# Second cross attention: heads scored in quads by row tiles, keys spread once a sequence, values in one block

## The chip, the core and the metric

The kernel runs on one core of a Trainium2 chip. The metric is the device time of one execution in microseconds (us): 3467.15 us is the median of three runs of the kernel before, from 3467.04 to 3475.69. TensorE (PE in the rows; PEld is its weight load), VectorE (DVE), ScalarE (ACT) and GpSimd (POOL) each run a queue of their own in order; they meet only at semaphores.

## The reference

A transformer decoder of two layers over 64 sequences of 128 tokens with 128 features. Six sublayers run one after the other, each on a layer norm of the residual x and added to x. The change touches the fifth, a cross attention with 16 heads of 8 features to a context of 77 positions per sequence, with a mask over the context:

```
x = x + L1_xattn(layernorm(x), ctx, ctx, mask, Wq, bq, Wk, bk, Wv, bv, Wo, bo)
# q = x @ Wq + bq; k, v = ctx @ Wk + bk, ctx @ Wv + bv; 16 heads of 8 features
# scores = q k^T / sqrt(8); masked positions get a very low score
# probs = softmax(scores); out = (probs v) @ Wo + bo
```

Everything is in 32-bit floating point.

## The kernel before

Each sublayer is a stage with a block of its own on every engine, and a barrier stands between stages. The stage of the change is `stage_context_attention`; its tiles have the prefix f_. It takes the 64 sequences one after the other (`over_sequences`: two steps, a loop of two steps a turn, four steps at the end), software-pipelined: step b works on sequence b, and prepares b+1, b+2 and b+3. Within a sequence the 16 heads are four groups of four: head 4g + u, with NG = 4 quads g and NU = 4 places u in a quad. Features 32g to 32g+31 belong to quad g.

For one group of four heads the kernel before does this, with n = 4b + u counting groups:

- `spread_keys` (GpSimd, line 2168) writes the keys of the sequence four times side by side, each copy zeroed outside the features of its head (`kx`, 128 x 308). One such instruction a group.
- `score` (TensorE, 1927 and 1929) puts the mask with an identity matmul in bf16 into a PSUM bank of `sc`, and adds q times the spread keys with a 32-bit matmul over all 128 features; a 32-bit matmul stands in the trace as two records. Two banks take turns.
- `lowest` (VectorE, 2023) finds the extreme of each head's row, `exponentials` (ScalarE, 2132) takes four exponentials with their sums, `invert` (VectorE, 2035) the reciprocal of the sums. The division is on GpSimd for even groups (`divide_even`, 2177), on VectorE for odd ones (`divide_odd`, 2042).
- `transposes` (TensorE, 1940) transposes the four heads into a bank of `tr`, of which there are two; `copy_probs` (ScalarE, 2141) copies it to SBUF; `values` (TensorE, 1951) multiplies by the values, in column tiles of 32, one group at a time.

Once a sequence there are also: `transpose_x`, `project_qk`, `project_v`, `project_out` (TensorE); `biases` (VectorE: the mask row `neg` 2000, `qT` 2002, `kT` 2006), `spread_values` (2015), `copy_out` (2051), `residual` (2056) and the layer norm of sequence b+3 (VectorE with GpSimd); `copy_xT` (ScalarE); `add_bias` (GpSimd).

The order on each engine is the order in which its `step` is written out by hand. A buffer that is used again is guarded by a wait on its last reader, for example `exponentials` of group n waits until the division of group n-2 has read `pr`.

Of the kernel before, what the change touches and what calls it, by code (L numbers as in the profile page):

```python
# [16 lines left out]
BF16 = mybir.dt.bfloat16  # L17
# [1806 lines left out]
def context_attention_weights(mem, w):  # L1824

    wT = mem.sbuf("wT", [128, 3, 128])
    woT = mem.sbuf("woT", [128, 128])
    bias = mem.sbuf("bias", [128, 2])
    bv = mem.sbuf("bv", [128, 128])
    bo = mem.sbuf("bo", [128, 128])  # L1830
    hsel = mem.sbuf("hsel", [128, H])
    mask = mem.sbuf("mask", [128, B, CK], I32)
    loads = [(wT[:], w["f_wT"]), (woT[:], w["f_woT"]), (bias[:], w["f_bias"]), (bv[:], bcast(w["f_bv"])),
            (bo[:], bcast(w["f_bo"])), (hsel[:], w["hsel"]),
            (mask[:].rearrange("p b k -> p (b k)"), bcast(w["mask"].rearrange("b k -> (b k)")))]
    return (wT, woT, bias, bv, bo, hsel, mask), loads


def stage_context_attention(nc, X, w, consts, tiles):
# [4 lines left out]

    KP = 96
    with ExitStack() as ctx:
        mem = Memory(nc, ctx, "f")
        wT, woT, bias, bv, bo, hsel, mask = tiles
# [8 lines left out]
        kx = mem.sbuf("kx", [128, 2, NU, NG, CK])  # L1857
        vx = mem.sbuf("vx", [128, 2, NU, 128])
        low = mem.sbuf("low", [128, 2, NG])
        sums = mem.sbuf("sums", [128, 2, NG])  # L1860
        rec = mem.sbuf("rec", [128, 2, NG])
        pr = mem.sbuf("pr", [128, 2, NG, CK])
        pn = mem.sbuf("pn", [128, 2, NG, KP])
        prT = mem.sbuf("prT", [128, 2, NG, 128])
        oT = mem.sbuf("oT", [128, 128])

        sc = mem.psum("sc", [128, 2, 512])
        tr = mem.psum("tr", [128, 2, 512])
# [12 lines left out]
        rec_made = mem.sem("rec_made")  # L1881
        pn_even, pn_odd = mem.sem("pn_even"), mem.sem("pn_odd")
        tr_made, prT_made = mem.sem("tr_made"), mem.sem("prT_made")
# [4 lines left out]
        with nc.Block() as block:  # L1888
# [10 lines left out]
            def _(pe):  # L1899
# [19 lines left out]
                def score(b, p, u):  # L1919
                    n = 4 * b + u  # L1920
                    if due(n - 1):
                        pe.wait_ge(exped, n - 1)
                    pe.wait_ge(neg_made, b + 1)
                    pe.wait_ge(qk_made, 2 * b + 2)
                    pe.wait_ge(kx_made, n + 1)
                    dst = sc[:, u % 2, 0:NG * CK]
                    pe.matmul(dst, consts.ident_bf[:], neg[:, p].unsqueeze(1).broadcast_to([128, NG, CK]),
                              start=True, stop=False)
                    pe.matmul(dst, qT[:, p], kx[:, p, u], start=False, stop=True).then_inc(scored, 1)

                def transposes(b, p, u):
                    n = 4 * b + u
                    if u % 2:
                        pe.wait_ge(pn_odd, 2 * b + u // 2 + 1)
                    else:
                        pe.wait_ge(pn_even, 2 * b + u // 2 + 1)
                    if due(n - 1):
                        pe.wait_ge(prT_made, n - 1)
                    for g in range(NG):
                        last = pe.transpose(tr[0:KP, u % 2, 128 * g:128 * g + 128], pn[:, u % 2, g], consts.ident[:])  # L1940
                    last.then_inc(tr_made, 1)

                def values(b, p, u):
                    pe.wait_ge(prT_made, 4 * b + u + 1)
                    if u == 0:
                        pe.wait_ge(vx_made, b + 1)
                        if due(b):
                            pe.wait_ge(oT_made, b)
                    for g in range(NG):
                        q = slice(32 * g, 32 * g + 32)  # L1950
                        last = pe.matmul(po[q, 0:128], vx[0:KP, p, u, q], prT[0:KP, u % 2, g],
                                         start=u == 0, stop=u == NU - 1, tile_position=(0, 32 * g))
                    last.then_inc(pv_made, 1)
# [7 lines left out]
                def step(b, p, last):  # L1961
                    if inside(b + 1):
                        project_v(b + 1, 1 - p)
                    for u in range(NU):
                        transposes(b, p, u)
                        if u == 0:
                            score(b, p, 3)
                        elif inside(b + 1):
                            score(b + 1, 1 - p, u - 1)
                        if u == 1 and inside(b + 2):  # L1970
                            transpose_x(b + 2, p)
                        if u == 2 and inside(b - 1):
                            project_out(b - 1)
                        if u == 2 and inside(b + 2):
                            project_qk(b + 2, p)
                        if u > 0:
                            values(b, p, u - 1)
                        elif inside(b - 1):
                            values(b - 1, 1 - p, NU - 1)
                    if last:  # L1980
                        values(b, p, NU - 1)
                        project_out(b)

                pe.wait_ge(ready, 3)
# [5 lines left out]
                for u in range(3):  # L1990
                    score(0, 0, u)
# [3 lines left out]
            def _(dve):  # L1995
                def biases(b, p):
# [7 lines left out]
                    if due(4 * b - 4):  # L2004
                        dve.wait_ge(kx_made, 4 * b - 4)
                    dve.tensor_scalar(kT[:, p], pf[:, 128:128 + CK], bias[:, 1:2], None, ALU.add).then_inc(qk_made, 1)

                def spread_values(b, p):
                    dve.wait_ge(v_made, b + 1)
                    if due(4 * b - 4):  # L2010
                        dve.wait_ge(pv_made, 4 * b - 4)
# [6 lines left out]
                def lowest(b, u):  # L2018
                    n = 4 * b + u
                    if due(n - 1):  # L2020
                        dve.wait_ge(exped, n - 1)
                    dve.wait_ge(scored, n + 1)
                    dve.tensor_reduce(low[:, u % 2], sc[:, u % 2, 0:NG * CK].rearrange("p (g k) -> p g k", g=NG),  # L2023
                                      AX.X, ALU.min).then_inc(low_found, 1)

                def invert(b, u):

                    n = 4 * b + u
                    if due(2 * b + u // 2):
                        if u % 2:  # L2030
                            dve.wait_ge(pn_odd, 2 * b + u // 2)
                        else:
                            dve.wait_ge(pn_even, 2 * b + u // 2)
                    dve.wait_ge(exped, n + 1)
                    dve.reciprocal(rec[:, u % 2], sums[:, u % 2]).then_inc(rec_made, 1)

                def divide_odd(b, u):
                    n = 4 * b + u
                    if due(n - 1):
                        dve.wait_ge(tr_made, n - 1)  # L2040
                    dve.wait_ge(rec_made, n + 1)
                    dve.tensor_tensor(pn[:, 1, :, 0:CK], pr[:, 1],
                                      rec[:, 1].unsqueeze(2).broadcast_to([128, NG, CK]), ALU.mult)\
                        .then_inc(pn_odd, 1)

                def copy_out(b):
# [3 lines left out]
                    dve.wait_ge(pv_made, 4 * b + 4)  # L2050
# [7 lines left out]
                def step(b, p, last):  # L2058

                    invert(b, 1)  # L2060
                    divide_odd(b, 1)
                    lowest(b, 3)
                    if inside(b - 1):
                        copy_out(b - 1)

                    invert(b, 2)
                    if inside(b + 3):
                        norm_statistics(dve, ln, X[:, b + 3], b + 3, 1 - p)
                    if inside(b + 1):
                        lowest(b + 1, 0)  # L2070
# [3 lines left out]

                    invert(b, 3)
                    divide_odd(b, 3)
                    if inside(b + 1):
                        lowest(b + 1, 1)
                    if inside(b - 1):
# [3 lines left out]

                    if inside(b + 1):
                        invert(b + 1, 0)
                        lowest(b + 1, 2)
                    if inside(b + 3):
                        dve.wait_ge(xT_made, b + 2)
                        norm_apply(dve, ln, X[:, b + 3], b + 3, 1 - p)
# [4 lines left out]
                dve.memset(vx[:], 0.0).then_inc(ready, 1)  # L2094
                dve.memset(pn[:], 0.0).then_inc(ready, 1)
                dve.tensor_scalar(allowed[:], mask[:], 0.0, None, ALU.not_equal).then_inc(ready, 1)
                dve.wait_ge(ready, 3)
# [11 lines left out]
                for u in range(3):  # L2109
                    lowest(0, u)  # L2110
                    if u == 0:
                        invert(0, 0)
# [3 lines left out]
            def _(act):  # L2116
# [6 lines left out]
                def exponentials(b, u):  # L2123
                    n = 4 * b + u
                    if due(2 * b + u // 2):
                        if u % 2:
                            act.wait_ge(pn_odd, 2 * b + u // 2)
                        else:
                            act.wait_ge(pn_even, 2 * b + u // 2)
                    act.wait_ge(low_found, n + 1)  # L2130
                    for g in range(NG):
                        op = act.activation(pr[:, u % 2, g], sc[:, u % 2, CK * g:CK * g + CK], ACT.Exp,  # L2132
                                            bias=low[:, u % 2, g:g + 1], scale=-1.0,
# [508 lines left out]
```

## Time and profile before

| | us |
|---|---|
| median of three runs | 3467.15 |
| the profiled execution | 3479.02 |
| span in the profile | 3477.2 |
| TensorE busy | 3171.6 (91%) |
| VectorE busy | 2570.1 (74%) |
| ScalarE busy | 2244.4 (65%) |
| GpSimd busy | 1567.5 (45%) |

The stage of the change stands between about 2600 and 3090 us of the span. The shares above are means over six stages, so the stage has to be read by itself: from its own stretch of the time line and its own groups. "Busy" joins the recorded durations; on TensorE the records of matmuls overlap and their ends are modelled, so the distance from one start to the next says more than the duration. In a row, "[0.62 <-PE f_sc L1929]" is the idle time of the engine ahead of the instruction and what ended it.

### The profile page before, as it was taken

The page shows a single profiled execution, that of the slowest core. Times are in us where ns is not written, and L with a number is a line of the kernel's source. Part 1 is how long each engine was busy: PE and PEld are TensorE (multiplying, and loading weights), DVE is VectorE, ACT ScalarE, POOL GpSimd, SP SyncE. Part 2 cuts the span into 40 slices and gives each one's busy share as a digit, 9 for nine tenths or more (in the row PEclk, how much of TensorE's full clock was granted, in tenths as well). Part 3 has the DMA queues.
Part 4 walks back from the last instruction along what each step waited for, and adds up shares of the span by engine and source line. Part 5 has one row for each costly group of instructions (what it writes and reads, how often), then busy time and mean ns, then how long its engine had stood idle before and what let it go on. Part 6 is the DMA issues. An engine that isn't in the chain of part 4 may idle for free. (4 is left out here: it accounts for less than half of the span.)

```text
span 3477.2 us, 97864 instructions
## 1 busy us (share of the span) xinstructions
PE 3171.6 (91%) x27203; PEld 2330.7 (67%) x27357; DVE 2570.1 (74%) x8326; ACT 2244.4 (65%) x8816; POOL 1567.5 (45%) x2572
## 2 busy tenths in 40 slices
PE   7999999899999999999999986879979999967776
PEld 4666666688888888888888864657756666644443
DVE  7888888577777777777777761126657888879997
ACT  6888888566666666666666652327758999952221
POOL 6888888312222222222222210016647777746665
PEclk9999999899999999999999998989999999977677
DMA  4000000100000000000000002220000000000000
GB/s 144 0 0 0 0 0 0 75 4 6 5 5 5 5 5 5 5 5 5 5 5 5 4 4 67 79 61 17 17 10 6 5 5 5 5 2 11 7 12 18
DMA packets 80366, 54.39 MB, mean 16 GB/s; under 512 B 24801, under 2 KB 74413, under 8 KB 80160
## 3 DMA queue, kind: packets, MB, share of 16 engines
q1 hardware_dynamic: 76192, 45.27, 4.6%
q0 software_dynamic: 4096, 8.16, 0.8%
q8 instruction: 39, 0.64, 0.1%
q14 instruction: 39, 0.32, 0.0%
HBM read 32.67 MB, written 20.97 MB: 15 GB/s over the span
## 5 line engine op out<-in xcount | busy, mean ns | idle before, releaser
L897 DVE COPY b_prT<-b_tr 128x512 f32<-128x512 f32 x512 | 352.2, 688 | 236.6 <-PE b_tr L789 232.3
L1155 ACT ACTIVATE b_pr<-b_sc,b_low 128x205 f32<-128x205 f32 x1024 | 430.3, 430 | 34.3 <-DVE b_low L873 34.3
L478 ACT ACTIVATE a_pr<-a_sc,a_low 128x128 f32<-128x128 f32 x1024 | 364.2, 381 | 37.2 <-POOL a_pn L522 26.3
L1212 POOL TENSOR_TENSOR b_ln_var<-b_ln_mean_var,all_eps 128x1 f32<-128x1 f32 x64 | 12.0, 187 | 756.6 <-DVE b_ln_mean_var L140 756.6
L888 DVE TENSOR_SCALAR b_pn<-b_pr,b_rec 128x205 f32<-128x205 f32 x1024 | 298.4, 334 | 54.8
L789 PE MATMUL b_tr<-all_ident,b_pn 128*128 128x128 f32 x2048 | 322.4, 280 | 5.3 <-DVE b_prT L897 3.1
L2132 ACT ACTIVATE f_pr<-f_sc,f_low 128x77 f32<-128x77 f32 x1024 | 319.1, 335 | 10.9 <-DVE f_low L2023 2.9
L513 POOL TENSOR_TENSOR a_kx<-a_qk,w_hsel 128x512 f32<-128x512 f32 x256 | 291.7, 1151 | 2.4 <-DVE a_qk L349 2.4
L789 PEld LDWEIGHTS b_tr<-all_ident,b_pn 128*128 128x128 f32 x2048 | 226.6, 140 | 86.9 <-issue 79.3
L265 PE MATMUL a_sc<-a_kx,a_qk 128*128 128x512 f32 x512 | 262.3, 594 | 11.7 <-POOL a_kx L513 9.2
L873 DVE TENSOR_REDUCE b_low<-b_sc 128x4 f32<-128x820 f32 x256 | 256.4, 1002 | 10.2 <-PE b_sc L777 10.2
L777 PE MATMUL b_sc<-b_kT,b_q 64*128 64x205 f32 x2048 | 247.0, 359 | 0.0
L478 ACT ACTIVATION_READ_ACCUMULATOR a_pr<-a_sc,a_low 128x1 f32 x1024 | 225.9, 221 | 0.0
L2132 ACT ACTIVATION_READ_ACCUMULATOR f_pr<-f_sc,f_low 128x1 f32 x1024 | 221.9, 217 | 0.0
L806 PE MATMUL b_pm<-b_prT,b_vt 128*64 128x128 f32 x2048 | 213.6, 284 | 8.3 <-issue 5.3
L276 PEld LDWEIGHTS a_tr<-all_ident,a_pn 128*128 128x128 f32 x1024 | 127.8, 141 | 135.0 <-issue 126.6
L1155 ACT ACTIVATION_READ_ACCUMULATOR b_pr<-b_sc,b_low 128x1 f32 x1024 | 208.6, 204 | 0.0
L806 PE MATMUL b_pm<-b_prT,b_vm 128*64 128x128 f32 x2048 | 202.2, 273 | 0.0
L487 ACT ACTIVATE a_prT<-a_tr 128x512 f32<-128x512 f32 x256 | 155.1, 606 | 67.9 <-PE a_tr L276 67.9
L367 DVE TENSOR_REDUCE a_low<-a_sc 128x4 f32<-128x512 f32 x256 | 173.6, 678 | 30.7 <-PE a_sc L265 30.2
L777 PEld LDWEIGHTS b_sc<-b_kT,b_q 64*128 64x128 f32 x2048 | 166.2, 186 | 43.7 <-issue 43.0
L1164 ACT ACTIVATE b_oT<-b_pm 128x256 f32<-128x256 f32 x256 | 97.5, 381 | 131.7 <-PE b_pm L806 130.3
(292 smaller groups left out, 8795.4 us busy)
## 6 DMA issues: line engine op xcount, KB each, us to landing
scratch_x<-b_zeros SPq DMA_DIRECT2D x12, 512.0 KB, 5.0
e_xr<-scratch_x SPq DMA_DIRECT2D x24, 256.0 KB, 3.0
scratch_y<-e_yr SPq DMA_DIRECT2D x24, 256.0 KB, 2.4
all_X<-in_x SPq DMA_DIRECT2D x8, 512.0 KB, 6.9
e_w<-in_e_w SPq DMA_DIRECT2D x16, 256.0 KB, 3.0
out_x<-all_X SPq DMA_DIRECT2D x8, 512.0 KB, 3.2
w_mask<-in_mask SPq DMA_DIRECT2D x1, 2464.0 KB, 9.8
b_cT<-in_ctxT SPq DMA_DIRECT2D x32, 77.0 KB, 2.0
```

Of the source, the lines that this page charges most:

```text
L265: pe.matmul(sc[:, u % 2], qk[:, p, 0], kx[:, p, u], start=False, stop=True).then_inc(scored, 1)
L367: dve.tensor_reduce(low[:, u % 2], sc[:, u % 2].rearrange("p (g k) -> p g k", g=NG), AX.X, ALU.min).then_inc(low_found, 1)
L478: op = act.activation(pr[:, u % 2, g], sc[:, u % 2, 128 * g:128 * g + 128], ACT.Exp, bias=low[:, u % 2, g:g + 1], scale=-1.0, accum_out=su ...
L513: pool.tensor_tensor(kx[:, p, u], qk[:, p, 1].unsqueeze(1).broadcast_to([128, NG, 128]), hsel[:, NG * u:NG * u + NG].unsqueeze(2).broadcas ...
L777: last = pe.matmul(sc[:, j % 2, h, KN * i:KN * i + KN], q[r, p, 2 * j + i], kT[r, p, 2 * j + i], start=True, stop=True, tile_position=(XD ...
L789: last = pe.transpose(tr[:, o:o + 128], pn[:, j % 2, 2 * i + h, 128 * t:128 * t + 128], consts.ident[:])
L806: last = pe.matmul(po[XD * h:XD * h + XD, 128 * i:128 * i + 128], v[:, p, f:f + XD], prT[:, j % 2, i, h, t], start=t == 0, stop=t == 1, ti ...
L873: dve.tensor_reduce(low[:, j % 2].rearrange("p (i h) -> p h i", h=2), sc[:, j % 2, :, 0:2 * KN].rearrange("p h (i k) -> p h i k", i=2), AX ...
L888: op = dve.tensor_scalar(pn[:, j % 2, g, 0:KN], pr[:, j % 2, g, 0:KN], rec[:, j % 2, g:g + 1], None, ALU.mult)
L897: dve.tensor_copy(prT[:, j % 2, i].rearrange("p h t q -> p (h t q)"), tr[:]).then_inc(prT_made, 1)
L1155: op = act.activation(pr[:, j % 2, g, 0:KN], sc[:, j % 2, h, KN * i:KN * i + KN], ACT.Exp, bias=low[:, j % 2, g:g + 1], scale=-1.0, accum_ ...
L2132: op = act.activation(pr[:, u % 2, g], sc[:, u % 2, CK * g:CK * g + CK], ACT.Exp, bias=low[:, u % 2, g:g + 1], scale=-1.0, accum_out=sums[ ...
```

## The change

In the new kernel the four heads that are worked on together are those of one quad g, so their features are one strip of 32 partitions.

- `score(b, p, half)` takes two quads at a time. Each quad is a row tile of 32 partitions with a PSUM bank of its own, four banks in all. The mask is added by a bf16 matmul over 32 partitions with a matrix `part` of 1/32.
- `spread_keys` runs once a sequence (`kx` is 128 x 308 for all four quads), with `own` in place of `hsel`.
- `transposes` writes into one bank `tr` instead of two. Its copy is on ScalarE for even quads (`copy_even`) and on VectorE for odd ones (`copy_odd`). `prT` holds all four quads of two sequences.
- `values` is one block of 16 matmuls a sequence, one step later than the transposes.
- All divisions are on GpSimd (`divide`).

The diff, cut to its core. On TensorE:

```diff
-                def score(b, p, u):
+                def score(b, p, half):
...
+                    for g in (2 * half, 2 * half + 1):
+                        q = slice(32 * g, 32 * g + 32)
+                        pe.matmul(sc[:, g, 0:NU * CK], part[q], neg[q, p].unsqueeze(1).broadcast_to([32, NU, CK]),
+                                  start=True, stop=False, tile_position=(32 * g, 0))
+                    for g in (2 * half, 2 * half + 1):
+                        q = slice(32 * g, 32 * g + 32)
+                        last = pe.matmul(sc[:, g, 0:NU * CK], qT[q, p], kx[q, p].rearrange("p u k -> p (u k)"),
+                                         start=False, stop=True, tile_position=(32 * g, 0))
+                    last.then_inc(scored, 2)
+                def transposes(b, g):
+                    n = 4 * b + g
+                    pe.wait_ge(normed, n + 1)
+                    if g % 2:
+                        pe.wait_ge(prT_even, n // 2 + 1 if isinstance(n, int) else 2 * b + g // 2 + 1)
+                    elif due(n):
+                        pe.wait_ge(prT_odd, 2 * b + g // 2)
...
                 def step(b, p, last):
+                    transposes(b, 0)
                     if inside(b + 1):
                         project_v(b + 1, 1 - p)
...
+                    if inside(b - 1):
+                        values(b - 1, 1 - p)
+                    transposes(b, 1)
+                    if inside(b + 1):
+                        score(b + 1, 1 - p, 0)
+                    transposes(b, 2)
+                    if inside(b + 2):
+                        transpose_x(b + 2, p)
+                    if inside(b + 1):
+                        score(b + 1, 1 - p, 1)
+                    transposes(b, 3)
+                    if inside(b - 1):
+                        project_out(b - 1)
+                    if inside(b + 2):
+                        project_qk(b + 2, p)
```

On VectorE, the copy that is new there (the step that calls it is shown as a queue below):

```diff
+                def copy_odd(b, p, g):
+                    if due(b - 1):
+                        dve.wait_ge(pv_made, b - 1)
+                    dve.wait_ge(tr_made, 4 * b + g + 1)
+                    dve.tensor_copy(prT[0:KP, p, g].rearrange("p u k -> p (u k)"), tr[0:KP]).then_inc(prT_odd, 1)
```

The step on ScalarE:

```diff
                 def step(b, p, last):
+                    exponentials(b, 2)
+                    copy_even(b, p, 0)
+                    exponentials(b, 3)
+                    if inside(b + 1):
+                        exponentials(b + 1, 0)
+                    copy_even(b, p, 2)
+                    if inside(b + 2):
+                        copy_xT(b + 2)
+                    if inside(b + 1):
+                        exponentials(b + 1, 1)
```

And the step on GpSimd:

```diff
                 def step(b, p, last):
+                    divide(b, 2)
                     if inside(b + 3):
                         norm_rsqrt(pool, ln, consts, b + 3, 1 - p)
+                    divide(b, 3)
+                    add_bias(b)
                     if inside(b + 1):
+                        divide(b + 1, 0)
                     if inside(b + 2):
+                        spread_keys(b + 2, p)
+                    if inside(b + 1):
+                        divide(b + 1, 1)
```

The guards follow the same pattern as before: `exponentials(n)` waits for `divide(n-2)`, `divide(n)` for the transposes of n-2, `transposes(n)` for the copy of n-1 out of `tr` (the wait above), `spread_keys(b)` for both `biases(b)`.

How this stands in the queues. First ScalarE before, the start of a step in the loop: exponentials of group 2, copy of 0, exponentials of 3, copy of 1.

```order
L2132 ACTIVATE f_pr,f_sums<-f_sc,f_low 128x77 x4
L2139 REGISTER_ALU
L2140 REGISTER_ALU
L2141 ACTIVATE f_prT<-f_tr 96x512
L2130 REGISTER_ALU
L2132 ACTIVATE f_pr,f_sums<-f_sc,f_low 128x77 x4
L2140 REGISTER_ALU
L2141 ACTIVATE f_prT<-f_tr 96x512
```

Now, the same place: exponentials (b, 2), copy (b, 0), exponentials (b, 3), exponentials (b+1, 0), copy (b, 2).

```order
L2126 ACTIVATE f_pr,f_sums<-f_sc,f_low 128x77 x4
L2132 REGISTER_ALU
L2134 ACTIVATE f_prT<-f_tr 96x512
L2123 REGISTER_ALU
L2124 REGISTER_ALU
L2126 ACTIVATE f_pr,f_sums<-f_sc,f_low 128x77 x4
L2123 ISA
L2124 REGISTER_ALU
L2126 ACTIVATE f_pr,f_sums<-f_sc,f_low 128x77 x4
L2134 ACTIVATE f_prT<-f_tr 96x512
```

Before, a copy stood behind each four exponentials; now the copy of quad 2 stands behind eight, the last four of which belong to the next sequence.

VectorE before, the end of a step's middle: division of group 3 (`f_pn`), `lowest`, `residual`, the three of `biases`, `invert` of the next sequence.

```order
L2042 TENSOR_TENSOR f_pn<-f_pr,f_rec 128x4x77
L2022 REGISTER_ALU
L2023 TENSOR_REDUCE f_low<-f_sc 128x4
L2056 ISA
L2056 TENSOR_TENSOR all_X<-f_pm,all_X 128x128
L1999 ISA
L2000 ISA
L2000 TENSOR_SCALAR f_neg<-f_allowed 128x77
L2002 TENSOR_SCALAR f_qT<-f_pf,w_bias 128x128
L2006 TENSOR_SCALAR f_kT<-f_pf,w_bias 128x77
```

Now, the end of a step: `copy_odd(b, 3)`, `lowest(b+1, 3)`, `invert(b+1, 1)`, `residual(b-1)` and `biases(b+2)`.

```order
L2042 COPY f_prT<-f_tr 96x512
L2027 TENSOR_REDUCE f_low<-f_sc 128x4
L2036 RECIPROCAL f_rec<-f_sums 128x4
L2054 ISA
L2054 TENSOR_TENSOR all_X<-f_pm,all_X 128x128
L2003 ISA
L2004 ISA
L2004 TENSOR_SCALAR f_neg<-f_allowed 128x77
L2006 TENSOR_SCALAR f_qT<-f_pf,w_bias 128x128
L2010 TENSOR_SCALAR f_kT<-f_pf,w_bias 128x77
```

The biases now stand behind a copy that needs the last transposes of the step.

GpSimd before, the end of a step: keys of b+1 (group 3), division of group 0 of b+1, keys of b+2 (group 0).

```order
L2168 TENSOR_TENSOR f_kx<-f_kT,w_hsel 128x308
L2175 REGISTER_ALU
L2176 REGISTER_ALU
L2177 TENSOR_TENSOR f_pn<-f_pr,f_rec 128x4x77
L2165 ISA
L2167 ISA
L2168 TENSOR_TENSOR f_kx<-f_kT,w_hsel 128x308
```

Now: `add_bias`, `divide(b+1, 0)`, `spread_keys(b+2)`, `divide(b+1, 1)`.

```order
L2178 TENSOR_TENSOR all_X<-all_X,w_bo 128x128
L2169 ISA
L2170 REGISTER_ALU
L2171 TENSOR_TENSOR f_pn<-f_pr,f_rec 128x4x77
L2160 ISA
L2162 ISA
L2163 TENSOR_TENSOR f_kx<-f_kT,w_own 128x308
L2170 REGISTER_ALU
L2171 TENSOR_TENSOR f_pn<-f_pr,f_rec 128x4x77
```

A division of the next sequence now stands behind the keys of the one after it.

## Rows read from the trace of the kernel before

**Rows 1.** A stretch: length, busy us of PE PEld DVE ACT POOL, clock, DMA.
```profile
2900.00:2950.00 50.00, 50.00 (x479) 34.45 (x479) 40.72 (x153) 49.04 (x253) 38.03 (x62) 1.00 0.03 6
```

**Rows 2.** Groups by line, 2700 to 2900 us; busy us, mean ns, idle before.
```profile
L2141 ACT ACTIVATE f_prT<-f_tr 96x512 f32<-96x512 f32 x110 | 66.7, 607 | 0.0
...
L2042 DVE TENSOR_TENSOR f_pn<-f_pr,f_rec 128x308 f32<-128x308 f32 x55 | 33.2, 604 | 5.7
```

**Rows 3.** Waits, 2700 to 2900 us; total us, times, longest us.
```profile
PEld f_po L1951 <- issue: 32.0, 83, 0.4
```

**Rows 4.** Timeline of TensorE, one sequence; start us, duration us, engine, line.
```profile
2802.04 0.64 PE L1940 MATMUL f_tr<-all_ident,f_pn 128*96 128x128 f32 x4
2802.52 0.30 PE L1927 MATMUL f_sc<-f_neg,all_ident_bf 128*128 128x308 bf16 x1
2802.66 0.68 PE L1929 MATMUL f_sc<-f_kx,f_qT 128*128 128x308 f32 x2
2803.27 0.43 PE L1951 MATMUL f_po<-f_prT,f_vx 96*32 96x128 f32 x8
...
2808.98 0.43 PE L1951 MATMUL f_po<-f_prT,f_vx 96*32 96x128 f32 x8
2809.34 0.42 PE L1940 MATMUL f_tr<-all_ident,f_pn 128*96 128x128 f32 x2
```

**Rows 5.** Timeline of ScalarE, a quad and its copy.
```profile
2803.89 0.33 ACT L2132 ACTIVATE f_pr<-f_sc,f_low 128x77 f32<-128x77 f32 x1
...
2805.10 0.59 ACT L2141 ACTIVATE f_prT<-f_tr 96x512 f32<-96x512 f32 x1
```

**Rows 6.** Timeline of VectorE, same sequence.
```profile
2803.37 0.48 DVE L2023 TENSOR_REDUCE f_low<-f_sc 128x4 f32<-128x308 f32 x1 [0.62 <-PE f_sc L1929]
...
2805.75 0.35 DVE L2051 TENSOR_SCALAR f_oT<-f_po,f_valid 128x128 f32<-128x128 f32 x1
2806.02 0.17 DVE L2035 RECIPROCAL f_rec<-f_sums 128x4 f32<-128x4 f32 x1
...
2808.46 0.48 DVE L2023 TENSOR_REDUCE f_low<-f_sc 128x4 f32<-128x308 f32 x1
2808.86 0.29 DVE L2056 TENSOR_TENSOR all_X<-f_pm,all_X 128x128 f32 x1
2809.09 0.41 DVE L2000 TENSOR_SCALAR f_neg<-f_allowed 128x77 bf16 x1
2809.43 0.34 DVE L2002 TENSOR_SCALAR f_qT<-f_pf,w_bias 128x128 f32<-128x128 f32 x1
2809.69 0.28 DVE L2006 TENSOR_SCALAR f_kT<-f_pf,w_bias 128x77 f32<-128x77 f32 x1
```

**Rows 7.** Timeline of VectorE before the loop, GpSimd idle.
```profile
2614.22 0.20 DVE L2000 TENSOR_SCALAR f_neg<-f_allowed 128x77 bf16<-128x77 f32 x1
```

**Rows 8.** Timeline of GpSimd, same sequence.
```profile
2802.83 0.70 POOL L2177 TENSOR_TENSOR f_pn<-f_pr,f_rec 128x308 f32<-128x308 f32 x1 [0.68 <-DVE f_rec L2035]
2803.49 1.36 POOL L2168 TENSOR_TENSOR f_kx<-f_kT,w_hsel 128x308 f32<-128x308 f32 x2
...
2808.76 0.70 POOL L2168 TENSOR_TENSOR f_kx<-f_kT,w_hsel 128x308 f32<-128x308 f32 x1
```

**Rows 9.** Timeline of TensorE in the SiLU attention stage (prefix d).
```profile
2451.55 1.14 PE L1562 MATMUL d_sc<-d_qx,d_qku 32*128 32x512 f32 x8
2452.63 1.08 PE L1574 MATMUL d_po<-d_at,d_vx 128*32 128x128 f32 x32
```

**Rows 10.** Timeline of VectorE in the first cross attention (prefix b).
```profile
1500.82 0.68 DVE L897 COPY b_prT<-b_tr 128x512 f32<-128x512 f32 x1
1501.42 0.16 DVE L882 RECIPROCAL b_rec<-b_sums 128x2 f32<-128x2 f32 x1
```

**Rows 11.** Stretches of the last stage (prefix g), columns as in rows 1.
```profile
3133.00:3136.00 3.00, 1.45 (x8) 1.10 (x9) 2.93 (x11) 0.72 (x4) 2.02 (x4) 1.00 0.00 0
3136.00:3139.00 3.00, 2.58 (x7) 1.25 (x6) 3.00 (x14) 0.79 (x3) 1.64 (x4) 0.56 0.00 0
```

More of the change, by code:

```diff
@@ L1847, in stage_context_attention @@
         mem = Memory(nc, ctx, "f")
-        wT, woT, bias, bv, bo, hsel, mask = tiles
+        wT, woT, bias, bv, bo, own, mask = tiles
         allowed = mem.sbuf("allowed", [128, B, CK])
@@ L1931, in transposes @@
[L1931 to L1940, printed above, removed]
-                    last.then_inc(tr_made, 1)
@@ L1943, in values @@
[L1943 to L1952, printed above, removed]
+                    pe.wait_ge(kx_made, b + 1)
@@ new lines, in score @@
+                    last.then_inc(scored, 2)
[6 more added lines that the diff above has]
+                        pe.wait_ge(prT_odd, 2 * b + g // 2)
+                    for u in range(NU):
+                        last = pe.transpose(tr[0:KP, 128 * u:128 * u + 128], pn[:, g % 2, u], consts.ident[:])
+                    last.then_inc(tr_made, 1)
@@ new lines, in values @@
+                def values(b, p):
+                    pe.wait_ge(prT_even, 2 * b + 2)
+                    pe.wait_ge(prT_odd, 2 * b + 2)
+                    pe.wait_ge(vx_made, b + 1)
+                    if due(b):
+                        pe.wait_ge(oT_made, b)
+                    for u in range(NU):
+                        for g in range(NG):
+                            q = slice(32 * g, 32 * g + 32)
+                            last = pe.matmul(po[q, 0:128], vx[0:KP, p, u, q], prT[0:KP, p, g, u],
+                                             start=u == 0, stop=u == NU - 1, tile_position=(0, 32 * g))
@@ L1961, in step @@
                 def step(b, p, last):
+                    transposes(b, 0)
                     if inside(b + 1):
                         project_v(b + 1, 1 - p)
[L1964 to L1979, printed above, removed]
+                    if inside(b - 1):
[13 more added lines that the diff above has]
+                        project_qk(b + 2, p)
                     if last:
-                        values(b, p, NU - 1)
+                        values(b, p)
                         project_out(b)
-                pe.wait_ge(ready, 3)
+                pe.wait_ge(ready, 4)
                 transpose_x(0, 0)
@@ L1989, in _ @@
                 project_qk(1, 1)
-                for u in range(3):
-                    score(0, 0, u)
+                score(0, 0, 0)
+                score(0, 0, 1)
                 over_sequences(pe, step, tail=4)
@@ L2058, in step @@
                 def step(b, p, last):
[L2060 to L2066, printed above, removed]
                     if inside(b + 3):
                         norm_statistics(dve, ln, X[:, b + 3], b + 3, 1 - p)
+                    invert(b, 2)
                     if inside(b + 1):
-                        lowest(b + 1, 0)
                         spread_values(b + 1, 1 - p)
@@ L2108, in _ @@
                 biases(1, 1)
[L2109 to L2112, printed above, removed]
+                for g in range(NG):
+                    lowest(0, g)
+                invert(0, 0)
+                invert(0, 1)
                 over_sequences(dve, step, tail=4)
@@ L2155, in _ @@
+                act.wait_ge(ready, 4)
                 copy_xT(0)
```

186 lines of the change are left out of this document (78 added, 108 removed).

## The prediction

> **What bounds the kernel now.** I read four views, in this order. First the stage's own stretch: in 50.00 us TensorE is busy 50.00 and ScalarE 49.04, VectorE only 40.72 and GpSimd 38.03, at a granted clock of 1.00, the 2.4 GHz level [rows 1]. Then the waits: the largest that names TensorE, 32.0 us in 200, has no releaser, only "issue", at most 0.4 us each [rows 3]; it stands ahead of the column tiles, after TensorE's own work. Then TensorE's time line: a sequence takes 2809.34 - 2802.04 = 7.30 us [rows 4], and its starts follow each other without a hole that another engine fills. So before, the stage is bound by TensorE's occupancy, with ScalarE close behind. Last the queues, written out by hand: they decide what the change does, because it shortens the work of the two full engines and also draws new waits between all four.
>
> **What is removed and added, as occupancy.** Per sequence, in us of TensorE, start to start. Removed: four scorings over the full array, 2802.52 to 2803.27 = 0.75 each, 3.00; four value blocks, 2808.98 to 2809.34 = 0.36 each, 1.44 [rows 4]. Added: two scorings of two row tiles. The SiLU stage shows four row tiles with 512 columns, eight records, in 1.14 us [rows 9]. One after another they would take four times one tile's two passes, which, scaled from the 308-column pair (0.68 us, of which about 0.51 is streaming) is about 3.4; so row tiles run side by side. For two tiles at 308 columns I take 0.14 for the mask and 0.68 plus 0.03 for the pair, 0.85, plus about 0.12 for the change of tiling: 0.97 each, 1.94. And one value block of 16 matmuls, 1.08 [rows 9] plus 0.05. New occupancy: 7.30 - 3.00 - 1.44 + 1.94 + 1.13 = 5.93. ScalarE keeps four times four exponentials at 5.10 - 3.89 = 1.21 [rows 5] and two copies at 0.61 [rows 2], 6.06, plus the small copy of x. VectorE had 40.72 of 50.00, 5.95 a sequence [rows 1]; it gives up two divisions of 0.60 [rows 2] and takes two copies of 0.60, start to start [rows 10]. GpSimd had 5.55; it loses three key spreads of 0.70 and gains two divisions of 0.70 [rows 8]. If occupancy alone set the time, a sequence would take about 6.1 us.
>
> **The wait that takes its place.** Occupancy is only a lower bound. Follow what the new queues make each engine wait for, from the transposes of quad 1 of sequence b on TensorE (time 0) to the same of b+1:
>
> - Transposes (b, 1) last 0.64 [rows 4]. A hop between engines costs 0.03 to 0.04: scores end at 2803.34, `lowest` starts at 2803.37, and ends at 3.85 just before the exponentials at 3.89 [rows 4 to 6]. I take 0.04, and 0.05 into TensorE.
> - VectorE: `copy_odd(b, 1)` 0.60 [rows 10], `copy_out` 0.27 (2805.75 to 2806.02) [rows 6]. `lowest(b+1, 0)` starts at 0.64 + 0.04 + 0.87 = 1.55. The scores of b+1, from 0.60 to 1.45, are ready by then; that path is level.
> - `lowest` 0.48 [rows 6], hop, exponentials (b+1, 0) from 2.07; 1.21 to 3.28. Only then comes `copy_even(b, 2)`, which stands behind them on ScalarE although its transposes were done at 2.1: 0.61 to 3.89.
> - There is one bank `tr`, so transposes (b, 3) wait for that copy: start 3.94, end 4.58. TensorE could have started them at about 3.1.
> - VectorE: `copy_odd(b, 3)` from 4.62 takes 0.60; then `lowest(b+1, 3)` 0.40 (2808.46 to 2808.86), `invert` 0.10 (0.17 long, overlapped), `residual` 0.23, `neg` 0.12, `qT` 0.26, `kT` 0.28 [rows 6]: done at 6.61. Projection and residual inputs are ready earlier, so this is a queue, not a wait.
> - GpSimd: hop 0.08, `spread_keys(b+2)` 0.66 start to start, and behind it in the same queue `divide(b+1, 1)`, 0.70 [rows 8]: done at 8.05. Transposes (b+1, 1) start at 8.10.
>
> Each step needs the one ahead of it in the same period, so no amount of running ahead shortens this ring: 8.10 us a sequence against 7.30. The other rings I walked are shorter: values (b), which wait for `residual(b-1)` through `project_v`, let the next transposes go at about 7.4; exponentials against divisions need 2.4 for two quads, 4.8. TensorE is then idle about 2.1 of 8.1 us, and the gain in its work is never seen.
>
> **Where I chose.** `neg` took 0.41 in the loop, 2809.09 to 2809.50 [rows 6], and 0.20 with GpSimd idle [rows 7]. In the loop GpSimd spread keys from 2808.76 to 2809.46 [rows 8], and `neg` ended just behind; in the new queues GpSimd has nothing to do at that point. I take 0.34 less 0.21, about 0.12 start to start; the other end is 0.34, +0.22 us a sequence, +14 in all. The Trainium skill, SBUF — State Buffer, "SBUF: two separate sides", says that the pair of ports shared by VectorE and GpSimd is an exclusive lock held for a whole instruction. By that rule the difference is a lock and not the addressing in the loop, and 0.12 is right; if it were the addressing, 0.34. Row tiles not side by side: the pair would take 0.51 more, `lowest` would start at 2.07 in place of 1.55, +33 in all. Hops at 0.03 or 0.08 in place of mine: 0.2 less or more, 12 either way. The mask matmul over 32 partitions I cost like the one over 128; a lower bound of zero leaves the ring where it is, because the VectorE path is level with it. `copy_odd` reads 96 partitions, the row 128; same width, same price. Head and tail of the stage: a longer last value block, fewer key spreads ahead of the first score; I take nothing, 2 us either way.
>
> **The sum.** 64 sequences x (8.10 - 7.30) = 51 us. The profiled execution (3479.02, span 3477.2) would become 3530; it ran 12 above the median, which becomes 3467 + 51 = 3518.
>
> **Rivals.**
>
> *TensorE's clock falls in this stage.* Now it streams without holes at the 2.4 GHz level; it would have pauses of up to 0.9 us and about 2.1 in 8.1. In the last stage the level drops: a stretch at 1.00 with 1.45 of 3.00 busy is followed by one at a mean of 0.56 [rows 11]. Against it: those holes are longer than the ones here. Price: at 1.2 GHz the streamed parts double; in the ring, scores ready at 2.6 in place of 1.55, and 0.4 on transposes (b, 3): a ring of 9.5, +141, 3608. For a third to half of the stage: 3550 to 3563.
>
> *Row tiles one after another*, so that the change doesn't do what it says: 3467 + 51 + 33 = 3551. Rows 9 speak against it.
>
> *Faster: occupancy sets the time after all.* The place is `copy_even(b, 2)` and transposes (b, 3). This decides from the point where the ring gets shorter than 7.30, so it would have to lose 0.8 us, for instance the whole wait of transposes (b, 3) (0.9) by scores and minima that come a quad earlier than I walk them. Then ScalarE's and VectorE's 6.1 to 6.5 bound: 64 x (6.1 - 7.30) = -77, 3390; with small waits up to 3440. For it: two engines at 98 to 100% lose a sixth of their work. Against it: every hop of the ring is an order or a guard in the code. The Trainium skill, TensorEngine Tiling (Array Packing), "PSUM Bottleneck", warns that tiling speeds up TensorE but not the emptying of PSUM, which may then become the bottleneck; by that rule the single bank and its 0.61 copy would hold the time up here, as in the ring.
>
> **How the numbers follow.** The ring as walked: 0.73, its own range 3503 to 3550. Clock: 0.12. Serial row tiles: 0.03. Faster: 0.09; no change, the ring just at 7.3: 0.03. What a measurement of this kernel tells from no change is about 0.3%, 10 us. Faster 0.09, within 0.03, slower 0.88. The predicted time is the ring's, 3518. For 8 in 10 the range goes from 3495 to 3580: it takes in the bounds above (3505 to 3557), part of the clock's case, and leaves out the faster one.
>
> **What would show it.** In the new profile: a sequence of about 8.1 us in the stage, TensorE no longer 100% busy there; transposes waiting on the ScalarE copy of `tr` (about 0.8 us, once a sequence) and on the GpSimd division (once, 0.6 or so); GpSimd waiting for `kT`; divisions following the key spread at 0.66; `neg` near 0.20; VectorE's largest wait the transposes. The stages around unchanged. The steps would be wrong if the transposes of quad 3 start right behind the scores, if the row-tile pair takes 1.3 us or more, if the clock leaves 1.00, or if divisions are released by `rec` and not by the queue.

## The result

The new kernel takes 3550.81 us, median of four runs (3541.54 to 3553.87), against 3469.34 for the kernel before (four runs, 3467.04 to 3475.69): a ratio of 1.0224, 95% interval 1.0206 to 1.0241. It is slower, by 81 us in the medians; 51 were forecast.

The profiled executions differ by 3549.16 - 3479.02 = 70.1 us. Cut at the first and the last `residual` of the stage (VectorE, `all_X<-f_pm`), in us:

| | ahead of the first | first to last | behind the last | clock of the three |
|---|---|---|---|---|
| before | 2633.8 | 454.2 | 389.2 | 0.98, 1.00, 0.69 |
| after | 2638.2 | 522.0 | 387.1 | 0.98, 0.94, 0.72 |

The loss is in the stage: 67.8 us between first and last sequence, 4.4 ahead of the first. What stands behind is the last stage. It took between 376.5 and 393.3 us in the profiles of this study, at a clock of 0.78 to 0.68, though no kernel changes it; single executions differ by some 10 us through it.

### The profile page after: what moved, and what is told of

It reads as the page before. It is cut to its first block and busy times, and to the rows that moved or that the text cites. A ratio compares the mean times of both kernels' runs of the same rounds, so it can differ in the third digit from the quotient of the medians.

```text
span 3547.3 us, 97374 instructions
## 1 busy us (share of the span) xinstructions
PE 3114.1 (88%) x27203; PEld 2292.4 (65%) x27357; DVE 2552.2 (72%) x8327; ACT 2188.3 (62%) x8688; POOL 1502.2 (42%) x2508
## 5 line engine op out<-in xcount | busy, mean ns | idle before, releaser
L1943 PE MATMUL f_tr<-all_ident,f_pn 128*96 128x128 f32 x1024 | 175.6, 298 | 121.6 <-ACT f_prT L2134 61.1
L1943 PEld LDWEIGHTS f_tr<-all_ident,f_pn 128*96 128x96 f32 x1024 | 109.5, 135 | 207.0 <-issue 150.8
L2171 POOL TENSOR_TENSOR f_pn<-f_pr,f_rec 128x308 f32<-128x308 f32 x256 | 176.7, 700 | 92.3 <-DVE f_rec L2036 64.1
```

The costliest lines, as they stand in the source:

```text
L1943: last = pe.transpose(tr[0:KP, 128 * u:128 * u + 128], pn[:, g % 2, u], consts.ident[:])
```

## The profile after

The stretch that answers to [rows 1], and one ahead of it; the columns are the same.

```profile
2800.00:2850.00 50.00, 37.55 (x418) 24.95 (x416) 34.13 (x132) 37.67 (x214) 27.49 (x50) 1.00 0.03 5
...
2900.00:2950.00 50.00, 40.56 (x414) 28.81 (x414) 33.63 (x128) 37.65 (x210) 26.45 (x47) 0.90 0.02 4
```

No engine is full any more: TensorE fell from 50.00 to 37.55 us busy in 50 at the same clock, ScalarE from 49.04 to 37.67. Every engine waits. The waits of 2700 to 2900 us, for [rows 3]:

```profile
...
DVE f_prT L2042 <- PE f_tr L1943: 41.2, 46, 1.6
POOL f_kx L2163 <- DVE f_kT L2010: 40.1, 17, 2.4
ACT f_pr L2126 <- POOL f_pn L2171: 27.0, 23, 1.3
PE f_tr L1943 <- ACT f_prT L2134: 22.9, 24, 1.0
...
PE f_tr L1943 <- POOL f_pn L2171: 11.9, 21, 0.7
```

Each engine waits for another, which is how a ring looks in this view. TensorE's time line over one period, from transposes (b, 1) to the same of b+1, for [rows 4]:

```profile
2808.17 0.64 PE L1943 MATMUL f_tr<-all_ident,f_pn 128*96 128x128 f32 x4 [0.72 <-POOL f_pn L2171]
2808.74 0.31 PE L1927 MATMUL f_sc<-f_neg,f_part 32*128 32x308 bf16 x2
2808.89 0.68 PE L1931 MATMUL f_sc<-f_kx,f_qT 32*128 32x308 f32 x4
2809.67 0.62 PE L1943 MATMUL f_tr<-all_ident,f_pn 128*96 128x128 f32 x4
...
2810.48 0.68 PE L1931 MATMUL f_sc<-f_kx,f_qT 32*128 32x308 f32 x4
2812.06 0.64 PE L1943 MATMUL f_tr<-all_ident,f_pn 128*96 128x128 f32 x4 [0.90 <-ACT f_prT L2134]
...
2814.64 1.08 PE L1955 MATMUL f_po<-f_prT,f_vx 96*32 96x128 f32 x32
2816.38 0.64 PE L1943 MATMUL f_tr<-all_ident,f_pn 128*96 128x128 f32 x4 [0.66 <-POOL f_pn L2171]
```

The pair of row tiles takes 0.68 with four records, as long as one full-height matmul of two records in [rows 4]: the tiles run side by side. TensorE is idle for 0.90 between the second scores and transposes (b, 3), which wait for the copy. ScalarE in the same period, the first of each four exponentials of b+1 and the copy, for [rows 5]:

```profile
2810.20 0.33 ACT L2126 ACTIVATE f_pr<-f_sc,f_low 128x77 f32<-128x77 f32 x1 [0.72 <-DVE f_low L2027]
...
2811.42 0.59 ACT L2134 ACTIVATE f_prT<-f_tr 96x512 f32<-96x512 f32 x1
2811.90 0.28 ACT L2118 ACTIVATE f_xT<-f_pf 128x128 f32<-128x128 f32 x1
```

VectorE, for [rows 6], and GpSimd, for [rows 8]:

```profile
2808.84 0.69 DVE L2042 COPY f_prT<-f_tr 96x512 f32<-96x512 f32 x1 [0.69 <-PE f_tr L1943]
2809.45 0.34 DVE L2049 TENSOR_SCALAR f_oT<-f_po,f_valid 128x128 f32<-128x128 f32 x1
2809.71 0.46 DVE L2027 TENSOR_REDUCE f_low<-f_sc 128x4 f32<-128x308 f32 x1
...
2812.81 0.69 DVE L2042 COPY f_prT<-f_tr 96x512 f32<-96x512 f32 x1 [1.04 <-PE f_tr L1943]
2813.42 0.46 DVE L2027 TENSOR_REDUCE f_low<-f_sc 128x4 f32<-128x308 f32 x1
2813.81 0.17 DVE L2036 RECIPROCAL f_rec<-f_sums 128x4 f32<-128x4 f32 x1
2813.89 0.26 DVE L2054 TENSOR_TENSOR all_X<-f_pm,all_X 128x128 f32 x1
2814.07 0.19 DVE L2004 TENSOR_SCALAR f_neg<-f_allowed 128x77 bf16 x1
2814.17 0.34 DVE L2006 TENSOR_SCALAR f_qT<-f_pf,w_bias 128x128 f32<-128x128 f32 x1
2814.43 0.29 DVE L2010 TENSOR_SCALAR f_kT<-f_pf,w_bias 128x77 f32<-128x77 f32 x1
```

```profile
2814.89 0.70 POOL L2163 TENSOR_TENSOR f_kx<-f_kT,w_own 128x308 f32<-128x308 f32 x1 [2.34 <-DVE f_kT L2010]
2815.55 1.36 POOL L2171 TENSOR_TENSOR f_pn<-f_pr,f_rec 128x308 f32<-128x308 f32 x2
```

The two divisions behind the key spread are one row of 1.36; the first of them, `divide(b+1, 1)`, is what releases the transposes at 2816.38. Start to start this period is 8.21 us; the next is 8.34, and so on in turn, mean 8.28, against 7.30. In 14 of the first 58 periods it is more, up to 8.79; together these add 5.1 us. There the granted clock drops, as one of the drops shows in steps of half a microsecond (columns as in rows 1):

```profile
2718.50:2719.00 0.50, 0.28 (x4) 0.00 (x0) 0.41 (x2) 0.50 (x5) 0.50 (x2) 1.00 0.00 0
2719.00:2719.50 0.50, 0.00 (x0) 0.00 (x0) 0.39 (x2) 0.50 (x3) 0.10 (x2) 1.00 0.00 0
2719.50:2720.00 0.50, 0.22 (x2) 0.24 (x3) 0.00 (x0) 0.50 (x5) 0.50 (x1) 0.76 0.00 0
2720.00:2720.50 0.50, 0.50 (x4) 0.48 (x3) 0.00 (x0) 0.50 (x6) 0.17 (x1) 0.50 0.00 0
```

TensorE stands still, waiting for the copy, and near the end of that wait the clock goes to 0.50, the 1.2 GHz level, until 2723.

## The experiments

All ratios are to the kernel before, run on the same chip, with the 95% interval in brackets; "period" is the distance between two sequences' residuals, and where two are given, odd and even steps differ. The theory is the ring of the prediction: the period is the time of one closed chain of waits through all engines. The rivals: the single bank `tr` alone, TensorE's occupancy or slow row tiles, and the clock. Falls of the clock are counted between 2640 and 3040 us of the profiled execution.

**ScalarE's order.** `copy_even(b, 2)` ahead of `exponentials(b+1, 0)`:

```diff
                     exponentials(b, 3)
+                    copy_even(b, p, 2)
                     if inside(b + 1):
                         exponentials(b + 1, 0)
-                    copy_even(b, p, 2)
```

> One change against the new kernel: on ScalarE copy_even(b, 2) stands ahead of exponentials(b+1, 0). Ring theory (the sequence time is the ring transposes(b,1) - lowest(b+1,0) - exponentials(b+1,0) - copy_even(b,2) - transposes(b,3) - copy_odd(b,3) - biases(b+2) - spread_keys - divide(b+1,1)): transposes of quad 3 no longer wait for the copy and start right behind the scores, about 0.85 us sooner; copy_odd(b,3) is then held by invert(b+1,0), which waits for exponentials that start 0.5 later, so the ring gets shorter by about 0.55: 7.7 us a sequence in place of 8.28, ratio to the kernel before about 1.008. Rival (the time comes from the clock, from slower row tiles or from contention, not from this order): stays at 1.022.

Measured: 3547.05, ratio 1.0197 (1.0174 to 1.0219), periods 8.28 and 8.34, where 1.008 was expected. A miss. The wait did go: transposes (b, 3) start right behind the scores. But VectorE shows what took its place:

```profile
2804.57 0.67 DVE L2042 COPY f_prT<-f_tr 96x512 f32<-96x512 f32 x1
2805.15 0.47 DVE L2027 TENSOR_REDUCE f_low<-f_sc 128x4 f32<-128x308 f32 x1
2805.91 0.18 DVE L2036 RECIPROCAL f_rec<-f_sums 128x4 f32<-128x4 f32 x1 [0.29 <-ACT f_pr L2126]
2806.12 0.29 DVE L2054 TENSOR_TENSOR all_X<-f_pm,all_X 128x128 f32 x1
```

`invert(b+1, 1)` now waits for exponentials (b+1, 1). ScalarE starts exponentials (b+1, 0) 0.7 later, not the 0.5 that was expected: 2.79 and 2.71 behind transposes (b, 1) in the two steps, where it was 2.03 and 2.11, because the copy ahead of them itself waits for transposes (b, 2). It copies `xT` and takes the next exponentials behind that. The ring has two branches between `lowest(b+1, 0)` and `invert(b+1, 1)`: through transposes (b, 3), and through ScalarE. The second was only about 0.4 shorter, and in this order it is the longer one. The clock did not fall in this kernel, and TensorE's longest wait was 0.76.

**GpSimd's order.** Both divisions of b+1 ahead of the key spread:

```diff
                     if inside(b + 1):
                         divide(b + 1, 0)
+                        divide(b + 1, 1)
                     if inside(b + 2):
                         spread_keys(b + 2, p)
-                    if inside(b + 1):
-                        divide(b + 1, 1)
```

> One change against the new kernel: on GpSimd divide(b+1, 1) stands ahead of spread_keys(b+2). Ring theory: the division goes as soon as its reciprocal is there and no longer waits for qT, kT and the key spread; what is late next is residual(b-1) - project_v - values - transposes(b+1,1): about 7.5 us a sequence, ratio 1.004. Rival: the order costs nothing, stays at 1.022.

Measured: 3510.52, ratio 1.0092 (1.0072 to 1.0112), and again on another chip 1.0101 (1.0082 to 1.0121). Periods 7.42 and 7.62, mean 7.52, with some near 8.0. One queue position is worth 0.75 us a sequence, three quarters of the loss in the period, and some 40 of the 81 us in the medians. The expected period (7.5) was right and the time was missed. The profiled executions show where: they differ by 34 us from the kernel before, 13 of them the period (58 x 0.22), 8 the falls of the clock, 8 the first and the last sequences, 4 the last stage. The repeat, expected:

> The divide-first kernel once more, on the same chip as the one with masks three times over: ratio 1.007 to 1.011 as before, sequences of 7.42 and 7.62 us with some near 8.0 where the granted clock falls to 1.2 GHz while TensorE waits for the copy of quad 2. If its falls were an accident of one execution, none now.

In the repeat the clock fell nine times, in the first execution eight times; it is no accident of one execution.

**Both orders together.**

> Both changes together. Ring theory: transposes of quad 3 early and the division out of the key spread's shadow; the next ring is exponentials(b+1,1) - invert(b+1,1) - residual(b-1) - project_v - values(b) - transposes(b+1,1), about 7.15 us a sequence, ratio 0.997. Rival: both gone and still 1.02, then the time is not in the waits.

Measured: 3489.75, ratio 1.0043 (1.0026 to 1.006), periods 7.45 and 7.58, granted clock 1.00. A miss again: the period is that of GpSimd's order alone, and the stage is shorter (467.7 us against 479.1): by 8.9 us in the first 58 periods, where the falls of the clock had cost 8.3, and by 2.6 in the last five. TensorE now waits for VectorE's `residual`, which stands behind `invert`:

```profile
PE f_pm L1916 <- DVE all_X L2054: 9.3, 26, 0.4
```

**And the residual.** On top of both orders, `residual(b-1)` right behind `copy_odd(b, 3)`:

```diff
                     copy_odd(b, p, 3)
+                    if inside(b - 1):
+                        residual(b - 1)
                     if inside(b + 1):
                         lowest(b + 1, 3)
                         invert(b + 1, 1)
-                    if inside(b - 1):
-                        residual(b - 1)
```

> As e3, and on VectorE residual(b-1) stands right behind copy_odd(b,3), ahead of lowest(b+1,3) and invert(b+1,1). Ring theory: project_v of the next step no longer waits, 6.4 to 6.6 us a sequence, ratio about 0.985: faster than the kernel before, near the occupancy of ScalarE and VectorE. Rival (occupancy of VectorE with its waits holds 7.2): as e3.

Measured: 3475.79 over ten runs, ratio 1.0009 (0.9997 to 1.0022), periods 7.15 and 7.22. As fast as the kernel before, and a miss by 0.6 us a sequence. The period is 0.1 shorter than before, but the first and the last sequences take 5 us more. ScalarE waits for transposes (b, 2) in order to copy them, which stands early in its queue now, and they stand behind transposes, a copy and scores. The chain passes the one bank twice, where transposes (b, 1) follow `copy_even(b, 0)` and where transposes (b, 2) follow `copy_odd(b, 1)`.

```profile
POOL f_pn L2171 <- DVE f_rec L2036: 59.4, 70, 1.0
ACT f_prT L2134 <- PE f_tr L1943: 29.7, 27, 1.1
...
2806.75 0.59 ACT L2134 ACTIVATE f_prT<-f_tr 96x512 f32<-96x512 f32 x1 [1.14 <-PE f_tr L1943]
```

**Two banks for `tr`**, with the queues of the new kernel. So that a bank is free, the projections of the values and of the output move into the bank of the attention output, which adds two waits on TensorE (for `oT_made` and `y_added`); the diff is cut to the transposes:

```diff
-        tr = mem.psum("tr", [128, 512])
+        tr = mem.psum("tr", [128, 2, 512])
...
-                    if g % 2:
-                        pe.wait_ge(prT_even, n // 2 + 1 if isinstance(n, int) else 2 * b + g // 2 + 1)
-                    elif due(n):
-                        pe.wait_ge(prT_odd, 2 * b + g // 2)
+                    if due(2 * b + g // 2):
+                        pe.wait_ge(prT_odd if g % 2 else prT_even, 2 * b + g // 2)
```

> The new kernel with its three queues as they are, but two banks for the transposes in place of one: each transposes waits for the copy of the one before last. (The values' and the output's projection move into the bank of the attention output, so that a bank is free.) Ring theory: transposes (b,3) no longer wait 0.9 us for the copy of quad 2, but the copy-first experiment showed a second branch of equal rank, exponentials (b+1,0), copy of x, exponentials (b+1,1), inverse (b+1,1), and the order on GpSimd is left: 7.9 to 8.2 us a sequence, 3510 to 3540, ratio 1.010 to 1.020. Rival, the single bank is the cause by itself (the two copies are then free to overlap and occupancy bounds): 6.1 to 6.6 us, ratio 0.97 to 0.99.

Measured: 3518.54, ratio 1.0141 (1.0119 to 1.0163), periods 8.03 and 8.09, clock 1.00: the ring theory's range, and far from the rival's. The single bank is not the cause by itself. The moved projection of the values waits 0.5 to 0.7, but transposes (b+1, 1) behind it still wait 0.67 for the division, so it isn't what sets the period. Transposes (b, 3) no longer wait, and `invert(b+1, 1)` waits for ScalarE again:

```profile
2804.45 0.18 DVE L2035 RECIPROCAL f_rec<-f_sums 128x4 f32<-128x4 f32 x1 [0.58 <-ACT f_pr L2125]
```

**Two banks, GpSimd's order and the residual**, ScalarE's queue as in the new kernel:

> Two banks for the transposes, both divisions of b+1 ahead of spread_keys(b+2) on GpSimd, and residual(b-1) right behind copy_odd(b,3) on VectorE; ScalarE's order is that of the new kernel. Ring theory: with the bank, the key spread and the minima out of the chain, what is left is ScalarE's 6.1 us of work with one or two small waits: 6.5 to 6.8 us a sequence against 7.30, 64 x -0.5 to -0.8 = -32 to -51, ratio 0.985 to 0.991, faster than both kernels. Rival, the clock falls once TensorE has pauses (it did in the new kernel in a quarter of the sequences): ratio 1.000 or more, with granted clocks under 0.95 in stretches. Rival, the pause between engines is worse than I count and the previous experiment's 7.2 us is a floor: ratio 0.999 to 1.001.

Measured: 3439.45 over five runs, ratio 0.9904 (0.9891 to 0.9918), periods 6.58 and 6.59. This beats both kernels: 33 us less than before, and 111 less than the new one, which ran on another chip. The same stretch as in [rows 1]:

```profile
2900.00:2950.00 50.00, 46.47 (x535) 32.28 (x535) 44.32 (x170) 46.60 (x270) 34.74 (x61) 1.00 0.03 6
```

TensorE's occupancy is 46.47 x 6.585 / 50 = 6.12 a sequence and ScalarE's 6.14, against the 5.93 and 6.06 that the prediction counted. The gain in work was real; it took three cuts of the ring to see it. Against the one-bank kernel with both orders and the residual two things differ: the second bank, and ScalarE's queue, where the copy of quad 2 stands behind exponentials (b+1, 0) again and ScalarE no longer waits ahead of it. What each gives by itself was not run.

**Is TensorE's work on the path?** The new kernel with the masks of the second pair of quads done three times over, in row tiles; the added results are overwritten:

```diff
                     for g in (2 * half, 2 * half + 1):
                         q = slice(32 * g, 32 * g + 32)
+                        for _ in range(2 * half):
+                            pe.matmul(sc[:, g, 0:NU * CK], part[q], neg[q, p].unsqueeze(1).broadcast_to([32, NU, CK]),
+                                      start=True, stop=True, tile_position=(32 * g, 0))
```

> The new kernel, and the mask matmuls of the second pair of quads done three times over (four more bf16 matmuls of 308 columns a sequence, in row tiles of 32 partitions, whose results are overwritten). They stand where TensorE waits for ScalarE's copy anyway. If TensorE's occupancy or row tiles that are slow had any part in the loss: 4 x 0.13 to 0.15 = 0.5 to 0.6 us more a sequence if the tiles follow one another, 0.3 if they run side by side, +17 to +38 us, ratio 1.028 to 1.034. Ring theory: the 0.9 us wait of transposes (b,3) shrinks by as much and nothing else moves: 0 to +5 us against the new kernel, ratio 1.021 to 1.025.

Measured: 3548.49, ratio 1.0209 (1.019 to 1.0228), periods 8.21 and 8.34, to 0.01 those of the new kernel.

```profile
2803.01 0.44 PE L1928 MATMUL f_sc<-f_neg,f_part 32*128 32x308 bf16 x4
2803.28 0.30 PE L1930 MATMUL f_sc<-f_neg,f_part 32*128 32x308 bf16 x2
2803.41 0.69 PE L1934 MATMUL f_sc<-f_kx,f_qT 32*128 32x308 f32 x4
2804.83 0.62 PE L1946 MATMUL f_tr<-all_ident,f_pn 128*96 128x128 f32 x4 [0.73 <-ACT f_prT L2137]
```

Four more matmuls cost 0.27 (two and two side by side), the wait shrinks from 1.00 to 0.73, and nothing else moves. TensorE's second scoring, its occupancy and its row tiles, is off the path. The first is so by less: in the new kernel its scores end at 2809.57, 0.14 ahead of `lowest(b+1, 0)`, which starts right behind `copy_out` on VectorE. One thing did change: the clock fell once, not 13 times.

**Work that makes it faster.** The same addition to the divide-first kernel, run beside its repeat:

> The divide-first kernel (both divisions of b+1 ahead of spread_keys(b+2) on GpSimd), and the mask matmuls of the second pair of quads done three times over, so that TensorE does 0.27 us of useless work a sequence ahead of its 1.0 us wait for ScalarE's copy. Theory on the clock: the 1.2 GHz stretches begin in that wait; in the divide-first kernel they cost 9 us (sequences of 7.86 to 8.13 in place of 7.42 and 7.62, 16 of 62). With the wait down to about 0.73 they are gone or nearly so, as in the new kernel with masks three times over (1 of 62): 5 to 9 us faster than the divide-first kernel run beside it, ratio 1.0065 to 1.008 where that one has 1.009. Rival, the falls have nothing to do with the pause, and work added is at best hidden: 0 to 3 us slower, and sequences near 8 us as many as before.

Measured: 3493.04 (six runs), ratio 1.0057 (1.004 to 1.0074), beside 3507.47 and 1.0101 for the same kernel without the useless work. The gain was put at 5 to 9 us; it is 14 in the medians and 9 in the profiled executions. The first and last residual are 469.5 apart, without it 480.8; one fall of the clock against nine. Of these 11 us, 7.8 lie in the first 58 periods, in the long ones. The rival, that the falls have nothing to do with the pause, is out. The edit makes the pause shorter and TensorE busier at once; the copy-first kernel has the work and the period of the new one, no wait above 0.76, and no fall, so a shorter pause alone is enough.

## Why the prediction was right, and where it was short

The time, 3551, lies in the range of 3495 to 3580, but by itself it speaks for no mechanism: it stands just above the ring's own range (3503 to 3550; a later sentence gives the same bounds as 3505 to 3557), and it is also the price of two rivals, serial row tiles (3551) and the clock (3550 to 3563). The profile tells them apart.

*The bound before* and *the ring*: right, step for step. Times from the start of transposes (b, 1), in us:

| | predicted | period at 2808.17 | the next, at 2816.38 |
|---|---|---|---|
| `lowest(b+1, 0)` starts | 1.55 | 1.54 | 1.61 |
| exponentials (b+1, 0) | 2.07 | 2.03 | 2.11 |
| `copy_even(b, 2)` | 3.28 | 3.25 | 3.32 |
| transposes (b, 3) | 3.94 | 3.89 | 4.06 |
| `copy_odd(b, 3)` | 4.62 | 4.64 | 4.78 |
| `kT` | 6.33 | 6.26 | 6.40 |
| `spread_keys(b+2)` | 6.69 | 6.72 | 6.85 |
| `divide(b+1, 1)` | 7.35 | 7.38 | 7.51 |
| transposes (b+1, 1) | 8.10 | 8.21 | 8.34 |

*The hop into TensorE* is the mis-sized term. I took 0.05, and 0.08 as the upper bound. Behind the division (0.70 long) it is 8.21 - 8.08 = 0.13 in both periods, and behind `copy_even` 0.05 in one and 0.15 in the other (3.32 + 0.59 = 3.91 to 4.06): the two steps of one turn of the loop don't start alike. With a few hundredths elsewhere that makes 8.28 in place of 8.10, 64 x 0.18 = 11 us, within the 12 that I allowed for hops.

*The clock stays at 1.00*: it did not, which I had named as a sign that the steps would be wrong; the steps held between the falls, and the rival at 0.12 came true in part. The 14 long periods add 5.1 us. The rival had named the pauses as the place, but priced them at 32 to 90 us beyond the ring, since I let the low level hold for a third of the stage or more. It held for 44 of the 400 us from 2640 to 3040.

*Head and tail, nothing*: the first sequence is done 4.4 us later.

*From the profiled execution to the median.* The sum in the profile is 51 + 11 + 5 + 4 = 71, and -2 behind the stage: 69, where 70.1 were measured. The medians differ by 81: the kernel before was profiled in an execution 10 above its median, the new one in an execution at its median. I carried the difference over unchanged, which was too simple. That the last stage's clock makes this spread is read from the profiles only.

*`neg` at 0.12*: its row is 0.19 long and the next instruction starts 0.10 behind it, where it was 0.41 and 0.34 in [rows 6]. GpSimd is idle there now; nothing in the addressing changed. The kernel with both orders shows the other case: a division starts 0.19 ahead of `neg`, which takes 0.57 and ends 0.06 behind it.

```profile
2804.17 0.70 POOL L2171 TENSOR_TENSOR f_pn<-f_pr,f_rec 128x308 f32<-128x308 f32 x1 [0.74 <-DVE f_rec L2036]
2804.36 0.57 DVE L2004 TENSOR_SCALAR f_neg<-f_allowed 128x77 bf16 x1
```

With the residual moved too, `neg` starts 0.03 ahead of the division and takes 0.20, and the division 0.73. The Trainium skill, SBUF — State Buffer, "SBUF: two separate sides", has VectorE and GpSimd locking each other out of a pair of ports for a whole instruction, where VectorE's instruction is in a 2-port mode or has two inputs in SBUF; by that rule the two should no longer meet in the new kernel. The traces agree, in that `neg` ends just behind GpSimd's instruction or takes its 0.19 to 0.20; whether `neg` is of these kinds, no run shows.

*Row tiles side by side*: right, and a little cheaper: a scoring, start to start of what follows it, is 0.79 in the copy-first kernel (2802.58 to 2803.37), where I took 0.97. Off the path, that saved nothing.

*The faster rival* described a kernel that is not this one. The version with two banks and new orders lands near its 6.1 to 6.5 us (6.58), and at the upper end of its times (3439 of 3390 to 3440). The Trainium skill, TensorEngine Tiling (Array Packing), "PSUM Bottleneck", warns that emptying PSUM may become the bottleneck once TensorE is sped up. The runs agree only in part: in the new kernel's own order the single bank was worth 0.2 (8.28 to 8.06), because the branch through ScalarE stood right behind it. With the queues in better order the period was 7.2 with one bank and 6.58 with two, but ScalarE's order differs between these kernels as well, so no run shows the bank's own share there. The prediction took the bank's 0.9 us as an example of what the ring would have to lose to be faster; it missed that second branch, and the first experiment showed it.

What stays open: why odd and even steps hop differently; what the second bank is worth in the better order; and how much the clock takes from this stage in executions that were not profiled. Of those only the mean clock of the whole kernel is known: 0.939 to 0.947 in the new kernel's four executions, of which the profiled one had 0.945.

## What to carry to other kernels

A change that takes work off full engines has to be walked as a cycle through all queues before its saving is counted: here 1.2 us less work a sequence came with a ring 1 us longer than the old period. When a ring is found, look for the branch right behind it, because taking away a wait of 0.9 to 1.0 us gave 0.2 or nothing where a parallel branch was 0.4 shorter. Look at queue positions first (one line moved on GpSimd gave 40 us), then at buffers, and keep going until an engine is nearly full.

## What the runs showed of the hardware

- TensorE's clock fell to 1.2 GHz in the middle of a stage in which its longest wait was 1.01 us. All 13 falls in the new kernel and all 17 in the two profiles of the divide-first kernel (2640 to 3040 us) began in the wait of transposes (b, 3) for ScalarE's copy, 0.91 to 1.01 us long, or at most 0.33 us behind its end. Each took the clock to 0.50. The kernels without this wait (copy first, both orders, with the residual, and those with two banks) had no wait above 0.76 us in their full periods and showed no fall there, and the two in which it was 0.73 showed one each.
- Useless matmuls ahead of a pause can pay: 14 us of 3507 in the divide-first kernel (3493.04 against 3507.47).
- Two row tiles of 308 columns in 32-bit took 0.68 us in the new kernel, the same as one full-height matmul in the kernel before; four more bf16 ones took 0.27 in the kernel that does its masks again.
- `neg` on VectorE took 0.19 us with GpSimd idle, 0.41 beside a key spread that had begun earlier (before), and 0.57 beside a division that had begun 0.19 earlier (both orders).
